# Attention outputs of two heads in one product, summed over a tile's sixteen heads in one PSUM bank

## The reference, cut to what matters

```python
q = (hidden_states @ q_proj_w.T).reshape(b, s, H, Q_DIM).transpose(0, 2, 1, 3)
compressed = hidden_states @ kv_a_proj_w.T
k_pass_lat, k_rot = compressed[..., :KV_RANK], compressed[..., KV_RANK:]
kv = _rmsnorm(k_pass_lat, kv_a_ln_w) @ kv_b_proj_w.T
...
scores = jnp.einsum('bhqd,bhkd->bhqk', q, k) * scaling
scores = jnp.where(causal[None, None], scores, NEG)
probs = jax.nn.softmax(scores, axis=-1)
out = jnp.einsum('bhqk,bhkd->bhqd', probs, v)
out = out.transpose(0, 2, 1, 3).reshape(b, s, H * V_DIM)
return out @ o_proj_w.T
```

## Time and profile before

| | |
|---|---|
| median of 3 runs | 820.64 us (820.28 to 822.99) |
| the profiled execution | 820.38 us |
| its span | 818.3 us |
| busy: TensorE, VectorE, ScalarE, GpSimd | 774.5, 556.4, 396.9, 271.6 us |
| granted TensorE clock, mean | 0.994 of full speed |
| output products (line 1735) | 256 instructions for 128 heads |
| scaled additions (line 1106) | 128 |

### The profile page before, as it was taken

How to read it: one execution, slowest core, us unless ns; L and a number is a source line. 1 busy time by engine, 2 the same in 40 slices (tenths; PEclk the granted TensorE clock), 3 DMA queues, 4 the chain that set the end, 5 groups by cost and what they waited for, 6 DMA issues and landing times.

```text
span 818.3 us, 16165 instructions
## 1 busy us (share of the span) xinstructions
PE 774.5 (95%) x4645; PEld 657.0 (80%) x4645; DVE 556.4 (68%) x1422; ACT 396.9 (49%) x898; POOL 271.6 (33%) x357
## 2 busy tenths in 40 slices
PE   8998989999999999999889999899989999999997
PEld 7887867777778788777779998798887778888786
DVE  5323778777878778777736666468857377777666
ACT  1234656655656566566414444313243266666531
POOL 2004446443434223231346665615423400000071
PEclk9999999999999999999999999999999999999999
DMA  7449971000000000019139899678631335555331
GB/s 213 102 109 344 404 286 42 28 28 28 28 22 22 22 22 22 21 34 333 66 98 312 300 365 353 226 280 274 240 111 61 121 99 154 155 154 154 109 97 64
DMA packets 62161, 120.74 MB, mean 148 GB/s; under 512 B 18192, under 2 KB 31760, under 8 KB 61968
## 3 DMA queue, kind: packets, MB, share of 16 engines
q1 hardware_dynamic: 51104, 95.41, 35.8%
q0 software_dynamic: 7680, 21.51, 7.3%
q10 hardware_dynamic: 3312, 3.02, 1.1%
HBM read 76.13 MB, written 43.78 MB: 147 GB/s over the span
## 4 chain that ended last, share of the span: by engine, by line
PE 72%; DVE 9%; issue 8%; POOL 5%; DMA 3%; ACT 3%; SPq 0%; DVEq 0%; ACTq 0%; POOLq 0%
PE scores L1598 9%; PE scores L1600 9%; PE scores L1599 9%; PE scores L1821 7%; PE acc_ps L2003 5%; PE misc_ps L1728 4%; PE misc_ps L1726 4%; PE probsT_ps L1713 3%; PE probsT_ps L1735 3%; PE scores L1831 3%; PE acc_ps L1713 3%; DVE xT_lo L1089 2%; POOL xd_d L770 2%; PE probsT_ps L1810 2%; DVE neg_max L1083 2%
## 5 line engine op out<-in xcount | busy, mean ns | idle before, releaser
L819 ACT ACTIVATE area<-scores,neg_max 128x128 f32<-128x128 f32 (+7 forms) x128 | 94.9, 742 | 86.5 <-DVE neg_max L1083 86.1
L1083 DVE TENSOR_REDUCE neg_max<-scores 128x1 f32<-128x128 f32 (+7 forms) x128 | 95.7, 750 | 21.9 <-PE scores L1685 21.8
L701 POOL DMA_INDIRECT xe_d<-x_rows,send_i x64 | 64.1, 1001 | 55.5 <-ACT x_rows L843 38.5
L731 POOL DMA_INDIRECT ye_d<-area,home_i x64 | 61.4, 959 | 41.2 <-issue 21.2
L1598 PE MATMUL scores<-kT_hi,weff_hi 128*128 128x512 f32 (+3 forms) x172 | 66.7, 388 | 2.2 <-issue 1.3
L1821 PE MATMUL scores<-area 128*96 128x128 f32 x512 | 66.7, 273 | 1.0 <-issue 0.6
L689 POOL CAST weff_hi<-area 128x256 fp32r<-128x256 f32 x42 | 17.0, 406 | 135.7 <-PE scores L1685 88.0
L1600 PE MATMUL scores<-kT_hi,weff_lo 128*128 128x512 f32 (+3 forms) x172 | 61.5, 358 | 0.0
L1599 PE MATMUL scores<-kT_lo,weff_hi 128*128 128x512 f32 (+3 forms) x172 | 61.5, 358 | 0.0
L1821 PEld LDWEIGHTS scores<-area 128*96 128x96 f32 x512 | 59.1, 163 | 2.1 <-issue 1.0
L776 POOL DMA_INDIRECT area<-yd_d,slot x16 | 15.2, 953 | 137.0 <-DMA yd_d<-area 132.4
(11 more groups left out here) (283 smaller groups left out, 2046.6 us busy)
## 6 DMA issues: line engine op xcount, KB each, us to landing
area<-w SPq DMA_DIRECT2D x23, 512.0 KB, 4.0
area<-gate_up SPq DMA_DIRECT2D x24, 384.0 KB, 4.5
xe_d<-area SPq DMA_DIRECT2D x8, 1088.0 KB, 11.4
area<-xe_d SPq DMA_DIRECT2D x31, 272.0 KB, 7.0
ye_d<-area SPq DMA_DIRECT2D x8, 1024.0 KB, 16.4
area<-ye_d SPq DMA_DIRECT2D x16, 512.0 KB, 5.1
area<-w SPq DMA_DIRECT2D x8, 1024.0 KB, 8.6
area<-down SPq DMA_DIRECT2D x24, 192.0 KB, 6.9
```

The lines of the kernel that those rows point to most:

```text
L701: pool.indirect_dma_start(xe_d, bass.IndirectOffsetOnAxis(send_i[:, t, k:k + 1], 0), x1_rows[:, t, :], None).then_inc(sent[k % 2] if t < T ...
L819: act.activation(row_of(n)[:, 0:L], score_bank(n)[:, 0:L], ACT.Exp, bias=neg_max[:, n % 4:n % 4 + 1], accum_out=rsum[:, s, k:k + 1]).then_ ...
L1083: dve.tensor_reduce(neg_max[:, n % 4:n % 4 + 1], score_bank(n)[:, 0:(n // HEADS + 1) * P], AX.X, ALU.max, negate=True).then_inc(max_ready, 1)
```

## The change

The outputs of a group are computed in another way. A context of four heads lies in one bank, 4 x 128 columns, with the high sum in partitions 0 to 63 and the low sum in 64 to 127. ScalarE (`swap_ctx`) now copies the low half of heads 0 and 1 and the high half of heads 2 and 3 to SBUF with the halves exchanged; VectorE (`sum_ctx`) adds them to what is in the bank, so that heads 0 and 1 come to lie in partitions 0 to 63 and heads 2 and 3 in 64 to 127 of one 128 x 256 tile; it then multiplies this tile with the inverse row sums. These have to lie along the columns: GpSimd (`spread_rinv`) spreads them over 64 columns each, and TensorE (`scale`) transposes that twice into a bank, a new tenant of the ring. `output` is now two products for a group, each of two heads, and all eight products of a tile are summed in the bank `acc_ps`, which VectorE reads once for a tile (`add_tile`). `wvo_copy` keeps only one half of the folded values, with the weights of two heads above each other.

The ring loses `acc_ps` and has 3, 2 and 6 banks instead of 4, 3 and 7. The scales are computed at place 0 of a group's eight and the outputs at place 3. The first context product of a group waits for the additions of the group before. Some semaphores are merged into one counter, and the loop that prepares `wvo` has two steps in a turn.

```diff
-TWO_OUTS = SHORT - 3 * QUAD
+TWO_OUTS = SHORT // QUAD - 3
+SCALE_AT, OUT_AT = 0, 3
...
-        LENT = pT + [acc, half[3]] + half[0:3]
-        long_rows = seat("out", TWO_OUTS)
+        LENT = pT + [half[3]] + half[0:3]
+        long_rows = seat("scale", TWO_OUTS)
...
-                banks_now = 4 if k < long_rows else 3 if k < tail else 7
+                banks_now = 3 if k < long_rows else 2 if k < tail else 6
...
+            def spread_rinv(G):
+
+                pool.wait_ge(rinv_done, G + 1)
+                if G >= 2:
+                    pool.wait_ge(scale_ready, G - 1)
+                pool.tensor_copy(spread[:, G % 2], rinv[:, G % 3, :].rearrange("p (m j) -> p j m", m=2).unsqueeze(3).broadcast_to(
+                    [P, 2, 2, RANK])).then_inc(rinv_spread, 1)
...
+            def swap_ctx(G):
+
                 act.wait_ge(ctx_step, blocks_to(G + 1))
-                if G >= 2:
-                    act.wait_ge(out_ready, QUAD * (G - 1))
-                act.copy(ctxT[:, G % 2, :], ctx_ps[:]).then_inc(ctx_copied, 1)
+                if G:
+                    act.wait_ge(ctx_summed, 2 * G)
+                act.copy(swapped[0:RANK], ctx_ps[RANK:, 0:HID]).then_inc(ctx_swapped, 1)
+                act.copy(swapped[RANK:], ctx_ps[0:RANK, HID:]).then_inc(ctx_swapped, 1)
...
+            def sum_ctx(G):
+
+                for part, rows in enumerate((slice(0, RANK), slice(RANK, P))):
+                    dve.wait_ge(ctx_swapped, 2 * G + 2)
+                    dve.tensor_tensor(halves_sum[rows], ctx_ps[rows, part * HID:(part + 1) * HID], swapped[rows],
+                                      ALU.add).then_inc(ctx_summed, 1)
+                dve.wait_ge(ctx_summed, 2 * G + 2)
+                dve.wait_ge(scale_ready, G + 1)
+                if G >= 2:
+                    dve.wait_ge(out_ready, G - 1)
+                dve.tensor_tensor(pair_ctx[G % 2], halves_sum, scale_of(G), ALU.mult).then_inc(ctx_scaled, 1)
+
+            def add_tile(t):
+
+                dve.wait_ge(out_ready, (t + 1) * SETS)
+                dve.wait_ge(ld_x, 32)
+                dve.tensor_tensor(x1[:, t, :], out_ps, x_in[:, t, :], ALU.add).then_inc(out_read, 1)
...
-                behind = n - 1 - 2 * QUAD
-                if 0 <= behind < TILES * HEADS:
-                    add_head(behind)
+                if i == 0 and 0 <= G - 2 < GROUPS:
+                    sum_ctx(G - 2)
+                if i == 2 and SETS - 1 <= G - 2 < GROUPS and (G - 2) % SETS == SETS - 1:
+                    add_tile(tile_of(G - 2))
...
+            def scale(G):
+
+                pe.wait_ge(rinv_spread, G + 1)
+                take_seat("scale", G)
+                for j in range(2):
+                    last = pe.transpose(scale_of(G)[:, j * P:(j + 1) * P], spread[:, G % 2, j].rearrange("p m r -> p (m r)"),
+                                        ident[:])
+                last.then_inc(scale_ready, 1)
+
+            def output(G):
+                g = G % SETS
+                pe.wait_ge(ctx_scaled, G + 1)
+                if G >= SETS and g == 0:
+                    pe.wait_ge(out_read, tile_of(G))
+                for j in range(2):
+                    last = pe.matmul(out_ps, pair_ctx[G % 2][:, j * P:(j + 1) * P],
+                                     wvo[:, (2 * g + j) * HID:(2 * g + j + 1) * HID], start=g + j == 0, stop=g + j == SETS)
+                last.then_inc(out_ready, 1)
...
             def pe_slot(G, i, n):
-                steps(G, 2 * i)
-                for m in heads_at(n):
-                    scores(m)
-                steps(G, 2 * i + 1)
-                if 0 <= G - 2 < GROUPS:
-                    output(QUAD * (G - 2) + i)
+                for place in (2 * i, 2 * i + 1):
+                    if place % 2:
+                        for m in heads_at(n):
+                            scores(m)
+                    if place == SCALE_AT and 0 <= G - 2 < GROUPS:
+                        scale(G - 2)
+                    steps(G, place)
+                    if place == OUT_AT and 0 <= G - 2 < GROUPS:
+                        output(G - 2)
```

More of the change, by code:

```diff
@@ L112, in build @@
         sgd = sb("sgd", [P, 2, BANK])
-        ctxT = sgd
+        swapped, halves_sum = sgd[:, 0, 0:HID], sgd[:, 0, HID:]
+        pair_ctx = [sgd[:, 1, u * HID:(u + 1) * HID] for u in range(2)]
         stats = sb("stats", [P, 6])
@@ L224, in build, with scale_of @@
         ctx_ps = misc
-        def out_of(n):
-            return seat_of("out", n)[:, 0:HID]
+        out_ps = acc[:, 0:HID]
+        def scale_of(G):
+            return seat_of("scale", G)[:, 0:HID]
         half = [banks[u][:, b * BANK:(b + 1) * BANK] for u in range(2) for b in range(2)]
@@ L402, in build @@
         tenants = []
-        for G in range(GROUPS + 1):
+        for G in range(GROUPS + 2):
             for spot in range(8):
+                if spot == SCALE_AT and G >= 2:
+                    tenants.append(("scale", G - 2))
                 if route_at(G, spot):
@@ L407, in build @@
                 tenants += [("block", b) for b in blocks_at(G - 1, spot)]
-                if spot % 2 and 0 <= G - 2:
-                    tenants.append(("out", QUAD * (G - 2) + spot // 2))
-        tenants += [("out", QUAD * (GROUPS - 1) + i) for i in range(QUAD)]
         tenants += [(what, TILES - 1) for what in route_places.values()]
@@ L1074, in _ @@
             split_keys(1)
-            wvo_copy(1)
-            with dve.Fori(2, PAIRS) as j:
-                split_weff(2 * j, 0, j)
-                split_weff(2 * j + 1, 1, j)
-                wvo_copy(j)
+            wvo_copy(1, 1)
+            with dve.Fori(1, PAIRS // 2) as i:
+                for odd in range(2):
+                    j = 2 * i + odd
+                    split_weff(2 * j, 0, j)
+                    split_weff(2 * j + 1, 1, j)
+                    wvo_copy(j, odd)
             def row_max(n):
```

105 lines of the change are left out of this document (45 added, 60 removed).

## The result

| | before | after |
|---|---|---|
| median of the runs | 821.55 us | 838.28 us |
| profiled execution, span | 820.38, 818.3 us | 836.6, 834.8 us |
| attention, first mask product to the end of the last output | 334.4 us | 349.9 us |

The changed kernel is slower: ratio 1.021, 95% interval 1.018 to 1.024. The forecast was 815.1 with a range of 802 to 827, so both the sign and the range were wrong. The difference between the two spans is 16.5 us, and 15.5 of it lies in the attention.

A forecast was written before the change was run, and what follows sets the result against it. TensorE was taken to set the pace, busy 308.5 of 323.7 us in layer 0's attention. Sum: 820.4 - 21.1 (TensorE's savings) + 23.8 (late bank) - 9 (waits given back) + 1 (rest) = 815.1 us; range 802 to 827.

The forecast's parts named there:

- what is given back: Attention: TensorE's 11.0 us of waits for VectorE's low halves mostly vanish, -9 us; at worst nothing returns.
- what TensorE loses: Attention: two outputs and two scale transposes replace four outputs, saving 0.66 us a group over 32 groups, -21.1 us.
- The bank term: Attention ring: block transposes wait for the scale's bank until VectorE's product ends, 1.85 us in two-bank slots, +23.8 us together.
- Rival 3: Attention outputs: each costs 0.24 us, not 0.43, so 9 us is saved and the time is 827; chance 0.05.
- What the other engines get: Attention, per group: ScalarE copies 0.74 us, VectorE relieved by 0.5 us, GpSimd copy 0.39 us at no cost.
- upper end: VectorE's two additions: a stop between them costs 0.15 twice a group in 19 groups, at most +5 us.
- What TensorE now waits for: Attention: the deciding term, block transposes waiting for the scale's bank behind VectorE's chain and product, +23.8 us, bounds +21 to +29.
- rival 2: Attention: late bank costs fully, nothing is given back, delay travels through the slot; 826 to 829 us, chance 0.20.
- the rest: Early tiles' variance and the attention's end, +0.5 for each of two early tiles and +0.5 at the end, rounded to +1 us.
- the slot is long beside its row maximum: nothing: Early slots, below groups 12 and 13: no TensorE wait for the scale's bank, 0 us.
- the first paragraph of the prediction: Layer 0's attention: TensorE sets the pace, so an instruction taken from it shortens the stretch nearly one for one.

The follow-up runs named there:

- e2: Changed kernel without the scale: no spread copy, no scale transposes, product multiplies by part of the input; 1.011 of before, attention 348.5 us.
- e1: Changed kernel with the scale out of the ring, in the unused half of the accumulators' bank, tile's sum left out; 1.003 of before, attention 341.6 us.
- e7: Changed kernel with the ring's third bank back, outputs taking a ring place, VectorE adding every group; 1.001 of before, attention 337.5 us.
- e8: Changed kernel with the third bank back, outputs in the ring and at place 5, addition a pass later; 0.996 of before, attention 332.5 us.
- e9: Changed kernel with outputs at place 5 and the tile's addition a pass later, ring as changed; 1.024 of before, attention 355.8 us.
- e12: e8 with VectorE's two additions run for the first group alone; 0.987 of before, attention 323.1 us.
- e4: Changed kernel with each group's two output products issued twice, 64 more products; 1.034 of before, attention 372.2 us.
- e10: e8 with ScalarE copying the scales to SBUF at the slot's head and the product a pass later; 1.000 of before, attention 335.7 us.
- e5: Changed kernel with scale transposes at place 6 of the slot before and scales copied to SBUF by ScalarE; 1.020 of before, attention 361.7 us.

## Why the prediction was wrong, step by step

Two terms of the sum failed, and one stood at nothing: "what is given back" (-9 us, 1.6 measured), "what TensorE loses" (-21.1 us, where its time outside waits fell by 12.9), and waits of outputs for the product (5.8 us). The bank term, +23.8 us, came true as a wait.

**What TensorE loses, -21.1 us: the price of an output right, the term too large by 8.2.** From start to next start, waits taken out, 128 outputs took 53.7 us before; after, 64 products take 27.1 (0.42 each) and 32 pairs of scale transposes 7.6 (0.24 a pair): -19.0 us. But by the same count the block transposes became dearer, 54.5 to 58.5, and the time after mask products 8.7 to 12.5 us. With contexts at -2.3 and 0.5 in the rest, only -12.9 of the 317.4 us outside waits is left. The busy times say the same (316.8 to 303.8). Some of the 8.2 may be the clock, see the last section. Rival 3, the output at 0.24, falls.

**What the other engines get: right.** The swap takes 0.37 + 0.365 us, an addition 0.421, the product 0.421, a tile's addition 0.39, GpSimd's spread 0.415; all within 0.04 of the values taken for them. Half the partitions cost the same as all. The two additions on different halves take 0.88 us together in the timeline, more than twice 0.421: in all 32 groups the second starts 0.03 us after the first has ended. Two instructions that both begin at partition 0 and do not wait for each other overlap instead:

```profile
366.46 1.23 DVE L1109 TENSOR_REDUCE neg_max<-scores 128x1 f32<-128x1024 f32 x1
367.61 0.69 DVE L1115 TENSOR_TENSOR xT_lo<-probsT_ps,xT_hi 128x512 fp32r<-128x512 f32 x1
```

The second starts at 367.61 and the first ends at 367.69, 0.08 us later. So there is a stop between the additions, of some 0.11 us a group; the sum had none, and its upper end 0.15 twice a group. By the Trainium skill, "VectorE: DVE Perf Modes", section on two Vector instructions with no wait between them, the second would be held until the first has finished; the trace agrees. The wait for one's own result that I had at 0.15 is short too: the product starts 0.03 us after the second addition.

**What TensorE now waits for, +23.8 us: right in size, wrong as a price.** 24.0 us were measured, 1.65 in the slot of the earlier trace rows for the 1.85 forecast. As a term of the sum it held; as the price of the late bank it does not. I asked only when the scale's bank comes back. e2 removes scale, bank and wait, and the time hardly moves; e1 removes the bank's wait and 8.2 us of attention. The rest stands as waits for low halves. The reading that fits is that a block now has two banks where it had three: its transposes, the high half behind an exponential, and the low half must be over before the block after the next can begin. In the prediction this stands as "before, the third bank back was that of an output or of a block", a remark on whose wait it is, without a price. The ring as a whole should have been priced: shorter ring and late bank together cost 12 us by e7 against after and 23 us by e8 against e9, of which e1 gives 8.2 to the late bank.

**What is given back, -9 us: wrong.** I let the 11.0 us of low-half waits vanish, because TensorE comes later. They are 10.0 us after, against 11.6 in the same stretch of before, so 1.6 came back. The shorter ring alone does not explain it: with the third bank back they are 14.5 and 13.8 us (e7, e8), and 11.4 still without the additions (e12). Why they stay is open. This is the step at which forecast and rival 2 part. Rival 2 had the mechanism (a block takes the bank of the block two before, the delay travels) and ended at 829, too low, because it priced it at 0.25 us in 8 to 20 slots.

**Not foreseen: 5.8 us of outputs that wait for the product.** In tiles 0 to 2 I had "the slot is long beside its row maximum: nothing". Block transposes wait 2.0 us there, and the outputs at place 3 another 3.8 us, in short slots. The other 2.0 us is one wait, of the last group's outputs, at the end of the attention (422.48 us), where "the rest" had +0.5. Tile 1, from its first mask product to that of tile 2, took 26.0 us after, 23.5 before. Two instructions of it, the second for normalised rows (1.66 us at the same place before):

```profile
104.58 1.13 PE L1776 MATMUL acc_ps<-area,sgd 128*128 128x256 f32 x4 [0.75 <-DVE sgd L1132]
...
108.99 0.44 PE L1784 MATMUL probsT_ps<-ident,x_rows 128*128 128x128 f32 x2 [2.02 <-DVE x_rows L1150]
```

And the last group's outputs:

```profile
422.48 1.13 PE L1776 MATMUL acc_ps<-area,sgd 128*128 128x256 f32 x4 [2.00 <-DVE sgd L1132]
```

So the early tiles gave nothing (tiles 0 to 2: 67.3 us before, 69.5 after), where 0.7 us a group, some 8 us, was forecast. Tiles 3 to 6 are 1.8 to 2.9 us longer each, tile 7 is 3.7.

**Where the saving went.** Against a forecast of -5.3 us for the profiled execution it was +16.2. The misses are 7.4 (low halves), 5.8 (outputs' waits), 5.5 (dearer transposes and masks, less the contexts), 2.1 (outputs and scales) and some 0.7 in the rest. With the third bank back (e8) the outputs save 20.4 us by starts, as forecast, and 14.6 of them are lost between first and second context product, mostly as waits for low halves (1.8 to 11.9 us). Before, outputs stood between the blocks and gave ScalarE and VectorE that time. That the missing cover is the cause of these 14.6 us is argued, not shown: e12 only excludes the additions. So the first paragraph of the prediction fails as well, that an instruction taken from TensorE shortens the stretch "nearly one for one": it holds for most of what is added (e4, 0.29 to 0.35 of 0.43) and did not hold for taking away (e2 against e1).

## What to carry to other kernels

- When a change takes a bank, a buffer or a slot out of a ring, price the ring first: the time from a writer's start to the last reader's end, over the number of banks, against the pace of the writer (block 0 in slot 29 after holds its bank from 362.09 to 365.34, 3.3 us, with two banks, and its transposes take 0.6). Do it for every tenant, not only for the new one that comes back late. That this sum gives the right size is not tested here.
- A wait that is named in the profile is the last of several. Taking its cause away shows the next one; only a run tells how far apart they are (24.0 us of waits removed, 1.3 and 8.2 us gained, in e2 and e1).
- Work that fills an engine may be the cover of a chain on two others. Before counting its removal as gain, ask what else is ready to run in its place.

## What the runs showed of the hardware

- The product (128 x 256, fp32) takes 0.414 us with both operands in SBUF (e10) and 0.421 us with one in PSUM (after). In e2, again with both in SBUF, the mean is 0.469 us: 26 of 32 take 0.424 to 0.427, and six take 0.55 to 0.90. Each of the six runs beside GpSimd's subtraction for the query split, and so do three long ones in e5:

```profile
158.38 0.72 POOL L699 TENSOR_TENSOR q_lo<-area,q_hi 128x256 fp32r<-128x256 f32 x1
158.49 0.90 DVE L1127 TENSOR_TENSOR sgd<-sgd,area 128x256 f32<-128x256 f32 x1
```

With one operand in PSUM (after) the same neighbour costs nothing:

```profile
141.27 0.72 POOL L701 TENSOR_TENSOR weff_lo<-area,weff_hi 128x256 fp32r<-128x256 f32 x1
141.35 0.42 DVE L1132 TENSOR_TENSOR sgd<-sgd,probsT_ps 128x256 f32<-128x256 f32 x1
```

- The granted clock fell inside the attention in after; in before it is 1.00 throughout. Four stretches of after (columns as above), in two pairs, each with a first part in which TensorE waited:

```profile
175.00:180.00 5.00, 3.20 (x20) 2.40 (x19) 3.07 (x9) 2.70 (x8) 1.92 (x3) 0.90 0.17 59
180.00:185.00 5.00, 5.00 (x28) 4.27 (x26) 3.76 (x13) 2.35 (x5) 1.48 (x4) 0.76 0.00 0
220.00:225.00 5.00, 3.38 (x20) 2.98 (x19) 2.55 (x7) 2.91 (x8) 2.12 (x3) 0.83 0.15 56
225.00:230.00 5.00, 5.00 (x30) 4.56 (x30) 3.84 (x12) 2.46 (x5) 0.00 (x0) 0.82 0.00 0
```

The second pair in before:

```profile
220.00:225.00 5.00, 3.52 (x25) 2.99 (x24) 3.96 (x12) 2.60 (x6) 2.12 (x3) 1.00 0.08 28
225.00:230.00 5.00, 5.00 (x32) 4.29 (x31) 3.74 (x9) 2.37 (x6) 1.12 (x2) 1.00 0.00 0
```

With nearly as much idle TensorE (3.52 of 5.00 us busy, against 3.38) its clock stays at 1.00. A mean of 0.76 is part of the time at 1.2 GHz; the four stretches together lack 0.69 x 5 = 3.5 us of full clock. So the lower clock can be up to 3.5 of the 15.5 us. That it follows from longer holes is not shown: e4 has fewer holes in its attention than after (38.6 against 46.0 us) and a lower clock, 0.97 against 0.99.
